# The second attention of a decoder layer: score, projection and scoring products of a head pair in one stretch, the product with v two pairs behind

## The reference, cut to what matters

```python
# B 8 batches, S 512 tokens, D 256, H 16 heads of 64, E 16 experts, 4 of them per token, float32
x = x + _L0_attn_ref(_layernorm(x), ...)                   # first attention, linear
def _L0_xattn_ref(q, k, v, Wq, bq, Wk, bk, Wv, bv, Wo, bo):  # second attention
    qh = (q @ Wq.T + bq).reshape(b, s, H, HD).transpose(0, 2, 1, 3)
    kh = (k @ Wk.T + bk).reshape(b, s, H, HD).transpose(0, 2, 1, 3)
    vh = (v @ Wv.T + bv).reshape(b, s, H, HD).transpose(0, 2, 1, 3)
    scores = jnp.einsum('bhqd,bhkd->bhqk', qh, kh) / np.sqrt(HD)
    scores = jnp.where(causal, scores, -jnp.inf)
    attn = jax.nn.softmax(scores, axis=-1)
    out = jnp.einsum('bhqk,bhkd->bhqd', attn, vh)
    return out.transpose(0, 2, 1, 3).reshape(b, s, H * HD) @ Wo.T + bo
x = x + _L0_xattn_ref(_layernorm(x), ctx, ctx, ...)
x = x + _L0_ffn_ref(_layernorm(x), ...)                    # top 4 of 16 experts per token
```

## Time and profile before

| what | us |
|---|---|
| median of three runs | 1517.63 (1517.53 to 1523.92) |
| the profiled execution, its own time | 1515.61 |
| its span in the profile | 1513.9 |
| PE / DVE / ACT busy in the span | 1456.3 / 1145.2 / 1074.3 |
| mean granted TensorE clock | 0.996 of full |

### The profile page before, as it was taken

The page is one execution under the profiler, slowest core; times in us unless marked ns, Lnnn a source line. Parts: engine busy times, 40 slices in busy tenths (PEclk is TensorE's granted clock), DMA queues, the critical chain, the costliest instruction groups (busy, mean ns, idle before and its releaser), DMA issues.

```text
span 1513.9 us, 33547 instructions
## 1 busy us (share of the span) xinstructions
PE 1456.3 (96%) x10859; PEld 1231.4 (81%) x10859; DVE 1145.2 (76%) x3498; ACT 1074.3 (71%) x2712; POOL 486.7 (32%) x401
## 2 busy tenths in 40 slices
PE   5999999999999999999999999998999999999997
PEld 4989777777776776777777777777999999999997
DVE  6888787778777778778777777778988666666663
ACT  5777686677677667667667667677776667676774
POOL 3344100002203203203103103004567764546476
PEclk9999999999999999999999999999999999999999
DMA  4221690360850951932902102047678886777785
GB/s 114 84 98 57 200 262 1 108 188 24 270 165 34 278 147 46 303 110 73 295 17 94 53 1 94 8 139 233 160 169 220 204 184 166 185 180 180 190 194 79
DMA packets 163355, 212.35 MB, mean 140 GB/s; under 512 B 16576, under 2 KB 125424, under 8 KB 163184
## 3 DMA queue, kind: packets, MB, share of 16 engines
q1 hardware_dynamic: 136176, 173.56, 38.3%
q0 software_dynamic: 26736, 36.65, 12.5%
q10 hardware_dynamic: 272, 0.00, 0.0%
HBM read 88.27 MB, written 121.90 MB: 139 GB/s over the span
## 4 chain that ended last, share of the span: by engine, by line
PE 81%; DVE 8%; ACT 6%; issue 2%; DMA 2%; POOL 0%; POOLq 0%; DVEq 0%; SPq 0%; ACTq 0%
PE ex_Y L1991 11%; PE ex_H L1971 10%; PE xa_work L1355 10%; PE xa_S L1385 8%; PE xa_work L1408 8%; PE xa_work L1398 7%; PE xa_work L1366 6%; PE xa_work L1425 6%; PE a_work L578 3%; ACT xa_prob L1507 3%; PE ex_X L1947 2%; ACT xa_probT L1520 2%; PE a_work L656 2%; DVE xa_prob L1636 1%; PE a_work L589 1%
## 5 line engine op out<-in xcount | busy, mean ns | idle before, releaser
L1507 ACT ACTIVATE xa_prob<-xa_prob,xa_nmax 128x512 f32<-128x512 f32 (+3 forms) x512 | 282.8, 558 | 51.1 <-DVE xa_nmax L1636 51.1
L1636 DVE CUSTOM_DVE_ANT_0 xa_prob<-xa_S,ahead_bits 128x512 f32<-128x512 f32 (+3 forms) x512 | 220.0, 486 | 37.4 <-PE xa_S L1385 37.3
L1991 PE MATMUL ex_Y<-experts_w_hi,ex_hT 128*128 x1144 | 216.1, 281 | 2.2 <-DVE ex_hT L2082 1.9
L1971 PE MATMUL ex_H<-ex_xT,ex_w 128*128 128x256 f32 x1536 | 199.2, 286 | 0.6 <-DVE ex_xT L2078 0.4
L1823 POOL DMA_INDIRECT expert_rows<-kept_xn,kept_rows x112 | 112.3, 1002 | 254.3 <-DVE xa_prob L1649 211.5
L1971 PEld LDWEIGHTS ex_H<-ex_xT,ex_w 128*128 128x128 f32 x1536 | 187.7, 191 | 1.0 <-issue 1.0
L1991 PEld LDWEIGHTS ex_Y<-experts_w_hi,ex_hT 128*128 128x128 f32 x1144 | 180.3, 188 | 3.8 <-issue 3.0
L2111 POOL DMA_INDIRECT out<-ex_y,ahead_bits x83 | 152.4, 1836 | 94.6 <-issue 31.7
L1649 DVE TENSOR_SCALAR xa_prob<-xa_prob,xa_sums 128x512 f32<-128x512 f32 (+3 forms) x512 | 169.9, 385 | 6.8
L1408 PE MATMUL xa_work<-xa_probT,xa_v 128*64 128x512 f32 (+3 forms) x1024 | 151.9, 439 | 9.8 <-DVE xa_q1lo L1626 6.7
L1991 PE MATMUL ex_Y<-experts_w_lo,ex_hT 128*128 x572 | 159.7, 279 | 0.0
(11 more groups left out here) (422 smaller groups left out, 3654.5 us busy)
## 6 DMA issues: line engine op xcount, KB each, us to landing
expert_rows<-xa_room_of_w_hi_and SPq DMA_DIRECT2D x256, 273.0 KB, 7.2
ahead_ctx<-in_w SPq DMA_DIRECT2D x31, 512.0 KB
ahead_x<-in_w SPq DMA_DIRECT2D x30, 512.0 KB, 4.4
kept_x<-expert_rows SPq DMA_DIRECT2D x44, 273.0 KB
ex_w_raw<-in_w SPq DMA_DIRECT2D x18, 512.0 KB, 4.8
experts_w_lo<-in_w SPq DMA_DIRECT2D x6, 1024.0 KB, 6.4
kept_xn<-expert_rows SPq DMA_DIRECT2D x20, 273.0 KB, 4.1
expert_rows<-xa_room_of_w_hi_and SPq DMA_DIRECT2D x38, 136.5 KB, 6.8
```

Of the source, the lines that this page charges most:

```text
L1507: m = act.activation(part, part, ACT.Exp, bias=nmax[n % 2][:, i, odd:odd + 1], scale=-1.0, accum_out=sums[n % 2][:, i, odd:odd + 1])
L1636: m = dve.tensor_tensor_reduce(prob[n % 2][:, odd, PROB_AT[i]:PROB_AT[i] + width], SB[slot[at]][:, odd, col:col + width], causal[:, S - wi ...
L1971: m = pe.matmul(bank[:, (f % 2) * ROWS:(f % 2 + 1) * ROWS], ww[:, c, f * P:(f + 1) * P], xx[:, c, :], start=(i == 0), stop=(i == len(terms ...
L1991: m = pe.matmul(YB[a][:, 0:D], hh[:, f, a * P:(a + 1) * P], W2[:, bass.ds(own * WE + f * D, D)], start=(i == 0), stop=(i == len(terms) - 1))
```

## The change

- In a pair, `project_k` and scores 1 follow scores 2 directly; then `project_v` and `output`, `project_q`, then `weigh` of pair **n - 2** (before: n - 1), and last the five turns of n - 1. The k step's low part is now a step of its own, `lower_k`, so that DVE takes it after `soften` of block 1.
- `weigh` no longer takes a bank of the ring but half of the score bank that block 1 of the running pair has just left (`SB[slot[at + 2, 1]]`); it waits for the first head's maximum there, and scores 2 of the next pair waits for `o_lo` of it. From `RING_FROM` = 61 on it uses the ring.
- The once-per-batch steps move: both `output` steps of a half stand together (p = 6 and p = 2), one pair later; `find3`, `find2`, `norm2`, `mark`, `place`, `lower_x`, `transpose_x` and `route` stand at the end of the pair, behind the turns and behind `even` of block 1. Two `project_v` stand at p = 5.
- The number of matmuls is the same: every step is there once.

```diff
--- before.py
+++ after.py
@@ -941,7 +941,7 @@
...
                 else:
                     w.wait_ge(kv_pe, done)
-                    leave_early("project_k", 0)
+                    leave_early("lower_k", 0)
                     leave_early("lower_q", 0)
...
@@ -1042,17 +1042,17 @@
 TRIANGLE = 1280
 TURNS = (((0, (2,)), (1, (2,))), ((0, (0,)),), ((0, (1, 3)),), ((1, (0,)),), ((1, (1, 3)),))
...
-V_LATE = {2: 0, 3: 1, 4: 2, 5: 3}
+V_LATE = {3: (0,), 4: (1,), 5: (2, 3)}
 V_EARLY = {0: 2, 1: 3}
-V_NEXT = {5: 0, 7: 1}
+V_NEXT = {6: 0, 7: 1}
...
 LOAD_W2 = ((2, 4), (4, 8), (14, 16), (0, 2), (12, 14), (8, 10), (10, 12))
 OF_LOAD = {e_: i for i, (first, last) in enumerate(LOAD_W2) for e_ in range(first, last)}
-LATE_MAX = (57, 59, 61)
+RING_FROM = B * PAIRS - 3
 FIRST_Q = ("project_q", 0)
...
 WO_IN_PAIR = {1: 0, 2: 1}
-TURN_AT, W2_IN_PAIR = 17, {61: (2, 3), 62: (4, 5)}
+TURN_AT, W2_IN_PAIR = 17, {61: (4, 5), 62: (2, 3)}
...
@@ -1071,63 +1071,56 @@
 def attention_plan():
     plan = [("begin", None), ("project_k", 0), ("project_v", (0, 0)), ("project_q", 0), ("project_v", (0, 1))]
     high_w2, low_w2 = ((lambda *mine, step=step: [(step, e_) for e_ in mine]) for step in ("high_w2", "low_w2"))
+    end = B * PAIRS - 1
     for n in range(B * PAIRS + 1):
         b, p = divmod(n, PAIRS)
         done, coming = b - 1, b + 1
         turns = [("turn", (n - 1, i)) for i in range(len(TURNS))] if n >= 1 else []
-        finish = [("weigh", n - 1), ("keep", n - 1)] if n >= 1 else []
+        weigh, keep = ([(step, n - 2)] if n >= 2 else [] for step in ("weigh", "keep"))
         sent = done if p == 7 else done - 1
-        scatters = [("scatter", (sent, i, min(n, B * PAIRS - 1), blk)) for i, blk in SCATTER_AT.get(p, ())] if sent >= 0 else []
-        if n == B * PAIRS:
-            plan += [*turns, *high_w2(15), *low_w2(15), *high_w2(6), *low_w2(6), *finish, *scatters]
+        scatters = [("scatter", (sent, i, min(n, end), blk)) for i, blk in SCATTER_AT.get(p, ())] if sent >= 0 else []
+        if n > end:
+            plan += [*turns, *high_w2(15), *low_w2(15), *high_w2(6), *low_w2(6), ("weigh", end), ("keep", end), *scatters]
             break
-        gap, behind_turns, first, ahead_of_max, middle, second = [], [], [], [], [], []
-        if b >= 1 and p in V_EARLY:
+        gap, first, high, low, extra, second = [], [], [], [], [], []
+        if p in V_EARLY:
             first.append(("project_v", (2 * b, V_EARLY[p])))
-        if p in V_LATE:
-            first.append(("project_v", (2 * b + 1, V_LATE[p])))
+        first += [("project_v", (2 * b + 1, t)) for t in V_LATE.get(p, ())]
...
-            gap += {2: [("find3", done)], 5: [("choose", done)], 6: [("weigh_gates", done)]}.get(p, [])
-            behind_turns += {3: [("transpose_x3", (done, 0))], 7: [("turn_gates", done)]}.get(p, [])
-            first += [("output", (done, 1, 0))] if p == 1 else []
-            middle += {2: [("norm3", done)], 4: [("route", done)], 5: [("mark", done)], 6: [("place", done)], 7: [("add_b2", (done, 0))] if coming < B else []}.get(p, [])
-            second += {1: [("output", (done, 1, 1))], 3: [("transpose_x3", (done, 1))]}.get(p, [])
-        if p == 5:
-            first.append(("output", (b, 0, 0)))
-            second.append(("output", (b, 0, 1)))
+            first += [("output", (done, 1, u)) for u in range(2)] if p == 2 else [("add_b2", (done, 0))] if p == 7 else []
+            gap += {3: [("norm3", done)], 5: [("choose", done)], 6: [("weigh_gates", done)]}.get(p, [])
+            extra += {3: [("transpose_x3", (done, c)) for c in range(KC)], 4: [("route", done)], 5: [("mark", done)]}.get(p, [])
+            second += [("find3", done)] if p == 2 else []
+        if done >= 1 and p == 0:
+            first += [("add_b2", (done - 1, 1)), ("store_x2", done - 1)]
+        if p == 6:
+            first += [("output", (b, 0, u)) for u in range(2)]
         if n in WO_IN_PAIR:
-            middle.append(("low_wo", WO_IN_PAIR[n]))
-            ahead_of_max.append(("high_wo", WO_IN_PAIR[n]))
-        if done >= 1 and p == 0:
-            middle += [("add_b2", (done - 1, 1)), ("store_x2", done - 1)]
+            high.append(("high_wo", WO_IN_PAIR[n]))
+            low.append(("low_wo", WO_IN_PAIR[n]))
         if coming < B:
-            gap += {3: [("find2", coming)], 4: [("lower_ctx", coming)]}.get(p, [])
-            second += {2: [("load", coming)], 3: [("split_ctx", coming)], 5: [("norm2", coming)],
-                       6: [(step, (coming, 1)) for step in ("transpose_x", "lower_x")]}.get(p, [])
-            ahead_of_max += [("transpose_x", (coming, 0))] if p == 6 else []
-            middle += [("lower_x", (coming, 0))] if p == 6 else []
-            second += [("project_v", (2 * b + 2, V_NEXT[p]))] if p in V_NEXT else []
+            first += [("project_v", (2 * b + 2, V_NEXT[p]))] if p in V_NEXT else []
+            gap += [("lower_ctx", coming)] if p == 4 else []
+            extra += [(step, (coming, c)) for step in ("transpose_x", "lower_x") for c in range(KC)] if p == 6 else []
+            second += {2: [("load", coming)], 3: [("find2", coming), ("split_ctx", coming)], 5: [("norm2", coming)]}.get(p, [])
         else:
-            second += {0: [("tables", 0)], 1: [("tables", 1)], 2: [("tables", 2), ("load_w2", 0)], 3: [("tables_turn", None)],
+            extra += [("tables_turn", None)] if p == 3 else []
+            second += {0: [("tables", 0)], 1: [("tables", 1)], 2: [("tables", 2), ("load_w2", 0)],
...
-        finish += [("add_b2", (done, 0))] if n == B * PAIRS - 1 else []
-        v_behind, v_ahead = ([("project_v", (0, t))] if n == 0 else [] for t in (2, 3))
-        in_front = 3 if n in LATE_MAX or coming < B and p in (4, 7) else 2
+        if done >= 0 and p == 6:
+            extra += [("place", done), ("turn_gates", done)]
         one, other = ([e_] for e_ in W2_IN_PAIR[n]) if n in W2_IN_PAIR else ([], [])
-        if n == B * PAIRS - 1:
-            plan += [("scores", (n, 3)), ("scores", (n, 2)), *turns[0:2], ("soften", (n, 3)), *turns[2:4], ("soften", (n, 2))]
-            plan += [("even", (n, 3)), *turns[4:], *behind_turns, *first, ("scores", (n, 1)), ("soften", (n, 1)), ("even", (n, 2)), finish[0]]
-            plan += [*high_w2(14), ("even", (n, 1)), *second, *finish[1:], *low_w2(14), *scatters]
+        plan += [("scores", (n, 3)), ("scores", (n, 2)), ("soften", (n, 3)), ("soften", (n, 2))]
+        if n == end:
+            plan += [*weigh, ("scores", (n, 1)), *keep, *turns, ("soften", (n, 1)), ("even", (n, 3)), ("even", (n, 2)), *first, *high_w2(14), ("even", (n, 1)),
+                     ("weigh", n - 1), ("keep", n - 1), *low_w2(14), *second, *scatters]
             continue
-        plan += [("scores", (n, 3)), ("scores", (n, 2)), *turns[0:2], *high_w2(*one), *turns[2:in_front], ("soften", (n, 3)), *turns[in_front:4], ("soften", (n, 2)), *v_behind]
-        plan += gap + [("even", (n, 3)), *low_w2(*one), *turns[4:], ("even", (n, 2))]
-        plan += [*behind_turns, ("project_k", n + 1)]
-        plan += [*first, ("project_q", n + 1)]
-        lower_q = [("lower_q", n + 1)]
+        plan += [("project_k", n + 1), ("scores", (n, 1)), ("soften", (n, 1)), ("lower_k", n + 1), *gap, *high_w2(*one), *first, ("project_q", n + 1)]
+        plan += [("even", (n, 3)), *low_w2(*one), ("lower_q", n + 1), ("even", (n, 2)), *high, *high_w2(*other), *weigh, *keep, ("even", (n, 1))]
...
-        plan += [*high_w2(*other), ("scores", (n, 1)), *ahead_of_max, ("soften", (n, 1)), *lower_q, *v_ahead, *low_w2(*other), *middle, ("even", (n, 1)), *second, *finish, *scatters]
-    b, end = B - 1, B * PAIRS - 1
+        plan += [*low, *low_w2(*other), *turns, *extra, *second, *scatters]
+    b = B - 1
...
@@ -1256,7 +1249,7 @@
                   "project_v": (v_ev, at), "turn": (t_ev, at), "weigh": (o_lo, at), "output": (x2_ev, at),
...
-            if (step, at) == FIRST_Q:
+            if (step, at) == FIRST_Q or step == "weigh" and at < RING_FROM:
                 continue
             elif (step, at) in ALONE:
...
@@ -1268,6 +1261,8 @@
         def bank(step, at):
             if (step, at) == FIRST_Q:
                 return SB[0][:, 0, :]
+            if step == "weigh" and at < RING_FROM:
+                return SB[slot[at + 2, 1]][:, 0, :]
             if (step, at) in alone_after:
                 return SB[0][:, 1, :]
             return work[bank_of[step, at] % len(work)]
@@ -1323,6 +1318,9 @@
             def work_bank(step, at):
                 if (step, at) == FIRST_Q:
                     return bank(step, at)
+                if step == "weigh" and at < RING_FROM:
+                    w.wait_ge(s_max, (at + 2, 1, 0))
+                    return bank(step, at)
                 if (step, at) in alone_after:
                     w.wait_ge(*alone_after[step, at])
                     return bank(step, at)
@@ -1375,6 +1373,7 @@
                 bank_pair = SB[slot[at]]
                 if at in before_in_slot:
```

(5 more changed lines are left out.)

## The result

The kernel before took 1519.94 us (median, 1517.53 to 1523.92), the changed kernel 1555.2 us (1551.04 to 1562.32): ratio 1.0211, 95% interval 1.0177 to 1.0245. It is slower by 1.8 to 2.4%, and the prediction (1517 us, range 1500 to 1533) missed it by 38 us. In the profiled executions the span went from 1513.9 to 1554.5 us.

A forecast was written before the change was run, and what follows sets the result against it. TensorE was taken to bound the kernel, busy 856.4 of 881 us in the second attention. Terms -36.5 + 14.4 + 17 + 5 = -0.1 on the profiled 1515.6 gave 1515.5, so 1517 us as median; range 1500 to 1533.

The forecast's parts named there:

- Changes of tile shape, 14.4 us: On TensorE in the second attention: 72 more switches between matmul tile shapes at 0.2 us each, +14.4 us.
- VectorE late for the last score block, 17 us: Block 1's scores wait for VectorE's maxima of block 3 behind once-per-batch steps: +17 us, bounds 0 and 30.
- a bare pair: Pair without once-per-batch steps on VectorE: 1.3 us to spare before block 1's scores, so no wait.
- The ring's waits removed, 36.5: TensorE's waits for work banks, 28.5 us of idle and 8 of short waits, all go: -36.5 us.
- 5 for start and end: First pairs wait for q's parts (about 2), last pairs for copies and a low part (3): +5 us, bounds 2 to 8.
- Nothing for DMAs and fills, "up to 2 if later norm3 met scatters": Loads, fills and scatters keep their pairs and queue order: no cost, up to 2 us if the later `norm3` met scatters.
- "DVE is never late": Maxima for block 1's scores start early enough, so the 17 us go: 1500 us; chance 0.20.
- "S1 waits in every pair, 1535": Block 1's scores, behind the k projection, wait in every pair as `keep`'s low part starts late: 1535 us; chance 0.22.
- "The ring waits come back elsewhere": K, v or q projections of p = 4 and 7 wait for x3 and x copies: +12 us, 1529; chance 0.07.
- "Weight loads are pulled ahead": TensorE's queue loads weights early across tile-shape changes where the order is new: -14.4 us, 1502; chance 0.03.

The follow-up runs named there:

- all three edits together: Changed kernel with q before the last score block, last batch's late v tiles one pair earlier, scatter gates apart: ratio 0.9960 (chip 3), 0.9957 (chip 10).

## Why the prediction was wrong

Its terms against what a chip without late signals shows (before to changed on chip 12, +12.7 us in the attention, from the ledger):

- **Changes of tile shape, 14.4 us.** Measured 14.9: 73 more, where 72 were counted, of the kinds that were named. Right. The Trainium skill (TensorEngine Tiling, Key Properties) says that changing the tiling mode drains the array; the traces agree, and the experiment with transposes between the score blocks shows 21.2 us for 123 more, with the time following less what waits absorb.
- **VectorE late for the last score block, 17 us.** Measured 20.8 at the junction of k and the last block. The places are those that were named, three a batch: 0.65, 1.22 and 0.72 us behind the pairs p = 2, 5 and 6, and a bare pair does not wait. Right, and q ahead of the block took them away.
- **The ring's waits removed, 36.5, and 5 for start and end.** Here the first step failed. Together they were to give 31.5 us back. All waits of before, junctions and inside, are 44.1 us; what is left after, without the 20.8 above, is 21.1. So 23.0 came back, 8.5 too few. The last batch is where it failed: it was to keep about 3 us ("at the end") and kept 13.0 of 13.1. Its longest wait is new. The load of expert weights, which waits for the last v tile, was moved nearer to its reader by the new places of the v tiles, and "start and end, 5" looked at the copies and not at the load; TensorE stands 5.9 us behind it, and the v tiles one pair earlier took that wait away. ScalarE's wait of 8.3 us stands in no row of before. The start cost 2.8 where about 2 was said.
- **Nothing for DMAs and fills, "up to 2 if later norm3 met scatters".** This is the step that failed by most. Of the 38.2 us that the attention lost on record, 25.4 (1086.0 - 1060.6) are not there when chip 12 runs the same program, and 23.3 not on chip 3. The ledger puts 9.3 of them at k to the last block, 7.7 at other junctions and 8.4 inside, half clock with them. I asked whether scatters would be late and not what else they disturb: the new order narrows VectorE's divisions, which are their gates, and so makes runs of six. That late signals go with the scatters is shown: the waits that end so all lie there, and moving the scatters moved them. That the length of the runs makes the loss is likely but not shown. With the gates apart the attention ended on chip 10 only 0.4 us later than on chip 3, where the changed order with its own gates lost 14.6 on chip 9; but these are two chips with the same time for the kernel before, not one, the changed kernel with its own gates wasn't run on chip 10, and all three edits together still lost 2.9 us there. By what path scatters hold up the signals of other engines stays open.

With the rivals: "DVE is never late" is out. "S1 waits in every pair, 1535" had the right sign and the wrong mechanism, as the bare pair does not wait. "The ring waits come back elsewhere" is true for the last batch alone. "Weight loads are pulled ahead" is out, as the new boundaries show their price. The same terms with the last batch read rightly would have given 1522.3 us on chip 12 (1513.9 - 0.1 + 8.5), and with the two terms that were right but small, 3.8 and 0.5 us short, 1526.6, where 1526.8 was measured. The late signals could not be read from the one trace of before, which came from an execution without them, but their place could: an instruction of a third engine whose gates the change moves.

## What to carry to other kernels

List the gates of every side activity (scatters, loads, fills) and look where the new order puts them: gates that were spread over a pair may fall together, and a load that waits for the last tile of something moves with that tile. Read the last batch apart: it has other neighbours, and waits that a change takes away everywhere else can stay there. And where a bank ring is short, an order with fewer changes of tile shape can cost much more than it saves (0.2 us saved in a pair, 1.5 us waited).

## What the runs showed of the hardware

- On two of four chips (9 and 10) signals of TensorE arrive late, by up to 3.8 us in the attention on record, in and up to 1.6 us behind runs of indirect DMAs on GpSimd, and several arrive in one burst; on chips 12 and 3 the same program shows none that ends a wait. The kernel before takes 1521.7 to 1522.3 us on the first two and 1513.4 to 1513.9 on the others.
- The traces of chips 9 and 10, and that of the changed kernel on record, have lost 14 to 18% of their semaphore records (15,382 to 16,123 of some 18,770). The Trainium skill (NOTIFIC — the notification-queue block, Overflow: three behaviours, one of which stalls the engine) says that a full record queue discards records or, set otherwise, stalls the engine that makes them. Discarding would fit the lost records, and stalling the delay, in which case the recording has a part in it. All executions here were recorded, so no run tells.
- Half clock comes behind waits of TensorE, but not behind each: after 2.2 us idle it ran 3.4 us at 1.2 GHz, after 5.8 us twice as long; behind the regular waits of 1.2 us it kept 2.4, and so it did in the kernel before behind this one of 2.4 us:

```profile
1030.63 2.37 PE L1408 MATMUL xa_work<-xa_probT,xa_v 128*64 128x512 f32 x16 [2.41 <-ACT xa_probT L1520]
```
